# The first cycle's order on GpSimd: rows scattered ahead of the scaling of the third pair

## The chip, the cores and the metric

The kernel runs on one core of a Trainium2 chip. A core has TensorE (PE), VectorE (DVE), ScalarE (ACT), GpSimd (POOL) and SyncE (SP), which run on their own and wait for one another on semaphores. The metric is the device time of one launch in microseconds; lower is better.

## What is computed

The input x has 16 images of 256 channels and 32x32 pixels. Two residual blocks follow one another, each on a group-normed x (in short):

```
x = x + L0(gn(x))      # mixture of small experts gives one scale per channel: x * sigmoid(...)
x = x + L1(gn(x))
L1: x_ssm, res, gate = split(silu(in_proj(x)))     # 768 x 256 matrix
    xf  = silu(conv3(x_ssm))                        # along the 1024 tokens
    dt, B, C = dbc(xf)                              # per head
    permute tokens by a Mobius-mapped order (per head); selective scan, 8 states; permute back
    out = silu(out_proj(y * silu(gate) + res))
```

L0 and both norms come down to one factor and one shift for each image and channel, so that the input of L1 is x * P + B in place. The order of the tokens depends on the head alone, and is computed at run time as a table of row numbers, `idx`.

## The kernel before

The 16 images are worked in 8 pairs (`PH = 8`, two images each). Three buffers hold pairs (`xb0` to `xb2`, pair i in `xb[i % 3]`). Each engine has its own program, written out by hand, and the order of instructions on an engine is the order of the code. There is no scheduler. After a prologue (statistics of all images, ranks of the tokens, the first pairs' projections) each engine runs `cycle(i)` for i from 0 to 7. Cycle i finishes pair i and prepares pairs i+1 and i+2. What it does around the change:

- POOL scales x of pair i+2 in place (`scale_x`, L443, two instructions per image). It needs the parameters of that pair (`pcur_ready`, set by DVE at L1027, `take_params`) and the loaded x (`x_in`). It signals `x_scaled` once per image.
- POOL scatters the rows of pair i+1 to DRAM in the permuted order (`scatter`, L462, 16 indirect DMAs of 128 rows of 290 floats). It needs `stage_ready`, which DVE gives with the last of three `add_bias` (L1046) on the tile `stage`, and the earlier reads of the same DRAM rows.
- `scattered` makes POOL wait until all the scattered rows have landed. SP waits for the same (`store_c`, L352), and then loads the permuted rows of pair i+1 back (`load_rows`, L362, L370, L372). DVE begins `softplus` (L1065) of pair i+1 from them.
- POOL gathers the results of pair i from DRAM in the original order (`gather`, L476, 8 indirect DMAs per head), after SP has stored that head's results (`store_y`, L389). PE turns them with `turn_back` (L1547).
- PE projects pair i+2 (`project`, L1429), first one image and then the other, and waits for `x_scaled` before each. Then come six of the eight units of `residual` of pair i (also L1429), `turn_back` of head 0 mixed with the last two units, `turn_back` of head 1 and the output projection (L1557).
- ACT drains the projection (L627) and applies the first tap (L634); DVE adds two more taps (`convolve`, L1040).

In cycle 0 alone the parameters of pairs 2 to 7 aren't there at its start. They are the end of a chain on DVE, PE and ACT (`rescaled`, `group_variance`, `scaled`, `biases`) inside cycle 0, which ends in `take_params(2)`. In a later cycle, `take_params` stands at the head of DVE's cycle.

Of the kernel before, what the change touches and what calls it, by code (L numbers as in the profile page):

```python
# [29 lines left out]
NB = 2  # L30
# [68 lines left out]
def build(nc, x_d, w1g_d, b1g_d, w2_d, b2_d, inw_d, inb_d, dww_d, dwb_d, dbcw_d, dbcb_d, alog_d,  # L99
          alogt_d, dpar_d, mob_d, outw_d, outb_d, const_d, out_d):  # L100
    with ExitStack() as ctx:
# [6 lines left out]
        def v(tensor, off, *dims, parts=P, p0=0):  # L108

            width = tensor.shape[1]  # L110
            assert off + sum(step * (count - 1) for step, count in dims) < width
            return bass.AP(tensor, p0 * width + off, [[width, parts]] + [list(d) for d in dims])
# [173 lines left out]
        def x_loads(i):  # L286

            return 16 * (1 + i // XB)
# [19 lines left out]
        def x_view(par, b, ct, off=0, n=N):  # L308
            return v(xb[par], (b * CT + ct) * N + off, (1, n))
# [113 lines left out]
        def _(pool):  # L423

            def hold(semaphore, value):

                if isinstance(value, int) and value <= 0:
                    return
                pool.wait_ge(semaphore, value)
                pool.sem_inc(pool_passed, 1)  # L430

            def scale_x(i, images=range(NB)):

                if i < NB:
                    hold(scales_ready, 1)
                else:
                    hold(pcur_ready, i + 1)
                par = i % XB
                for b in images:
                    hold(x_in[par][b], x_loads(i))  # L440
                    params = v(pcur, (par * NB + b) * PRM_W, (1, PRM_W))
                    for ct in range(CT):
                        last = nc.gpsimd.tensor_scalar(x_view(par, b, ct), x_view(par, b, ct),  # L443
                                                       params[:, PRM_P + ct:PRM_P + ct + 1],
                                                       params[:, PRM_B + ct:PRM_B + ct + 1], ALU.mult, ALU.add)
                    last.then_inc(x_scaled, 1)

            def scatter(i):
                for nt in range(NT):

                    if nt % BIAS_TILES == 0:

                        hold(stage_ready, i * BIAS_U + 2 + nt // BIAS_TILES)
                    if nt == 0:

                        hold(dbc_rows_in, 16 * (1 + H) * i)
                        for h in range(H):
                            hold(x_rows_in[h], 16 * i)
                        hold(c_stored, 16 * i)
                    for h in range(H):  # L460
                        k = h * NT + nt
                        pool.indirect_dma_start(  # L462
                            out=xt_d.ap(), out_offset=bass.IndirectOffsetOnAxis(ap=idx[:, k:k + 1], axis=0),
                            in_=v(stage, (nt * H + h) * ROW, (1, ROW)), in_offset=None).then_inc(rows_scattered, 16)

            def scattered(i):
                hold(rows_scattered, 256 * (i + 1))

            def gather(i, h):
                hold(y_stored[h], 48 * (i + 1))  # L470
                if h == 0:

                    hold(w_ready, H * (i + 1))
                for nt in range(NT):
                    k = h * NT + nt
                    pool.indirect_dma_start(  # L476
                        out=v(crow, k * NB * P, (1, NB * P)), out_offset=None, in_=yt_d.ap()[0:(h + 1) * N],
                        in_offset=bass.IndirectOffsetOnAxis(ap=idx[:, k:k + 1], axis=0)).then_inc(y_gathered[h], 16)
                if h == H - 1:
                    hold(y_gathered[0], 128 * (i + 1))  # L480
                    hold(y_gathered[1], 128 * (i + 1))

            def cycle(i):
                if i < PH - 2:
                    scale_x(i + 2, (0,))
                if i < PH - 1:
                    scatter(i + 1)
                if i < PH - 2:
                    scale_x(i + 2, (1,))
                if i < PH - 1:  # L490
                    scattered(i + 1)
                for h in range(H):
                    gather(i, h)
# [39 lines left out]
            for i in range(PH):  # L533
                cycle(i)
# [1182 lines left out]
```

## Time and profile before

| | us |
|---|---|
| median of 3 runs (lowest, highest) | 838.59 (837.87, 839.11) |
| the profiled execution, its own time | 842.28 |
| its span | 840.5 |
| PE busy in the span | 735.4 (88%) |
| DVE busy | 592.7 (71%) |
| ACT busy | 508.6 (61%) |
| POOL busy | 354.4 (42%) |

The span runs from the first instruction to the last. Cycle 0 lies at about 120 to 235 us. From 245 us on the cycles repeat every 88 us, and PE is busy for 85.3 of them. Issuing instructions of DMAs count as busy on POOL alone. Times in the rows below are us from the start of the span, and a number in brackets is idle time ahead of the row and what ended it. A fp32 matmul of 512 columns has two records in the trace, so that one image's projection (4 units of 2 matmuls) stands as x16 and six units of the residual as x24.

### The profile page before, as it was taken

How to read it: one execution, taken by the hardware profiler on the slowest of the kernel's cores; microseconds unless marked ns; L12 is line 12 of the kernel's file. 1: busy time of each engine (PE TensorE's matmuls, PEld its weight loads, DVE VectorE, ACT ScalarE, POOL GpSimd, SP SyncE). 2: the span in 40 equal slices, each digit the busy share in tenths (PEclk: the TensorE clock that was granted, in tenths of full speed). 3: DMA queues.
4: the chain of work that ended last, by engine and by line, in shares of the span. 5: the costliest groups of instructions: out<-in, count | busy, mean ns of one | idle time of the engine just before them, and what ended most of it. 6: DMA issues, size and time to landing. Idle time of an engine off the chain costs nothing.

```text
span 840.5 us, 11680 instructions
## 1 busy us (share of the span) xinstructions
PE 735.4 (88%) x4190; PEld 435.9 (52%) x4190; DVE 592.7 (71%) x1097; ACT 508.6 (61%) x954; POOL 354.4 (42%) x325
## 2 busy tenths in 40 slices
PE   2599867929999999999999999999999999697976
PEld 1356556614566456545755565546654566354642
DVE  5699589624787578957894779577957786378533
ACT  5775745426764875488467756676667764544422
POOL 2295300377038711873087407760577037600330
PEclk9699857969999999999999999999999999998989
DMA  9924550248464937484747564765568434942332
GB/s 329 369 101 165 143 128 1 83 134 212 107 213 144 245 87 246 136 215 120 219 143 189 164 183 156 190 194 131 195 191 213 115 131 142 254 114 87 110 92 100
DMA packets 128539, 136.40 MB, mean 162 GB/s; under 512 B 57305, under 2 KB 107106, under 8 KB 126434
## 3 DMA queue, kind: packets, MB, share of 16 engines
q1 hardware_dynamic: 114448, 99.42, 41.3%
q0 software_dynamic: 12288, 35.80, 13.1%
q10 hardware_dynamic: 1746, 0.45, 0.3%
q8 instruction: 33, 0.54, 0.3%
q14 instruction: 24, 0.20, 0.1%
HBM read 83.08 MB, written 53.61 MB: 163 GB/s over the span
## 4 chain that ended last, share of the span: by engine, by line
POOL 28%; PE 20%; DMA 19%; DVE 15%; issue 13%; ACT 4%; SPq 0%; POOLq 0%; DVEq 0%; ACTq 0%
POOL xt_scratch L462 15%; POOL crow L476 11%; DMA out<-xb 7%; PE pj L1557 7%; PE pj L1429 5%; DMA xb<-in_x 3%; DMA crow<-yt_scratch,idx 3%; DMA xt_scratch<-stage,idx 3%; DVE xf L1040 2%; DVE rs L894 2%; PE tp L1547 2%; POOL xb L443 2%; DMA crow<-cd_scratch 1%; PE tp L1449 1%; DVE xb L1225 1%
## 5 line engine op out<-in xcount | busy, mean ns | idle before, releaser
L1429 PE MATMUL pj<-xb,inw 128*128 128x512 f32 x768 | 350.4, 608 | 21.5 <-POOL xb L443 16.0
L1429 PEld LDWEIGHTS pj<-xb,inw 128*128 128x128 f32 x768 | 144.7, 194 | 187.2 <-issue 155.9
L462 POOL DMA_INDIRECT xt_scratch<-stage,idx x128 | 152.0, 1188 | 80.9 <-issue 73.7
L476 POOL DMA_INDIRECT crow<-yt_scratch,idx x128 | 135.0, 1054 | 109.5 <-DMA yt_scratch<-rs 62.1
L443 POOL TENSOR_SCALAR xb<-xb,pcur 128x1024 f32<-128x1024 f32 x30 | 46.5, 1559 | 257.2 <-DMA xb<-in_x 170.3
L1040 DVE SCALAR_TENSOR_TENSOR xf<-xs,small,xf 128x1024 f32<-128x1024 f32 x64 | 83.9, 1322 | 76.0 <-ACT xf L634 74.5
L1557 PE MATMUL pj<-gt,outw 128*128 128x512 f32 x256 | 118.9, 596 | 0.1
L734 ACT ACTIVATE rs<-pj,small 128x512 f32<-128x512 f32 x64 | 44.2, 694 | 58.1 <-PE pj L1557 58.0
L677 ACT COPY stage<-tp 128x256 f32<-128x256 f32 x128 | 47.8, 374 | 44.9 <-PE tp L1451 42.1
L690 ACT COPY rs<-pj 128x512 f32<-128x512 f32 x64 | 33.0, 600 | 67.7 <-PE pj L1524 67.7
L703 ACT ACTIVATE gt<-pj,pcur 128x512 f32<-128x512 f32 x64 | 41.5, 687 | 46.0 <-PE pj L1429 45.9
L1449 PE MATMUL tp<-dw,xf 128*128 128x162 f32 x256 | 63.3, 331 | 4.8 <-ACT stage L678 3.9
L1557 PEld LDWEIGHTS pj<-gt,outw 128*128 128x128 f32 x256 | 46.6, 192 | 38.2 <-issue 37.4
L1225 DVE SCALAR_TENSOR_TENSOR xb<-xb,pcur,rs 128x1024 f32<-128x1024 f32 x32 | 41.0, 1284 | 35.2 <-ACT rs L734 35.2
L1449 PEld LDWEIGHTS tp<-dw,xf 128*128 128x128 f32 x256 | 46.5, 204 | 36.5 <-issue 26.8
L627 ACT ACTIVATE xs<-pj,pcur 128x512 f32<-128x512 f32 x64 | 41.7, 688 | 37.5 <-PE pj L1429 30.3
L1169 DVE TENSOR_TENSOR big<-big,crow 128x1024 f32<-128x1024 f32 x32 | 60.6, 1938 | 1.1 <-DMA crow<-cd_scratch 1.0
L1451 PE MATMUL tp<-dw,xf 128*128 128x162 f32 x256 | 59.6, 317 | 0.0
L1212 DVE TENSOR_TENSOR gt<-tp,gt 128x512 f32<-128x512 f32 x64 | 41.2, 683 | 25.9 <-PE tp L1547 25.8
L724 ACT ACTIVATE rs<-pj,pcur 128x512 f32<-128x512 f32 x56 | 36.1, 687 | 28.9 <-PE pj L1429 24.7
L1547 PE MATMUL tp<-dw,crow 128*128 128x128 f32 x256 | 36.9, 286 | 15.9 <-DMA crow<-yt_scratch,idx 13.0
L665 ACT ACTIVATE big<-sg,small 128x272 f32<-128x272 f32 x128 | 50.1, 502 | 0.2
(256 smaller groups left out, 1059.0 us busy)
## 6 DMA issues: line engine op xcount, KB each, us to landing
xb<-in_x SPq DMA_DIRECT2D x16, 1024.0 KB, 5.7
xp<-xt_scratch SPq DMA_DIRECT2D x16, 1024.0 KB, 9.6
crow<-cd_scratch SPq DMA_DIRECT2D x16, 1024.0 KB
out<-xb SPq DMA_DIRECT2D x16, 1024.0 KB, 6.4
yt_scratch<-rs SPq DMA_DIRECT2D x16, 512.0 KB, 3.6
yt_scratch<-rs SPq DMA_DIRECT2D x32, 256.0 KB, 5.4
gt<-in_x SPq DMA_DIRECT2D x4, 1024.0 KB, 12.0
big<-in_x SPq DMA_DIRECT2D x4, 1024.0 KB, 13.7
```

Of the source, the lines that this page charges most:

```text
L443: last = nc.gpsimd.tensor_scalar(x_view(par, b, ct), x_view(par, b, ct), params[:, PRM_P + ct:PRM_P + ct + 1], params[:, PRM_B + ct:PRM_B ...
L462: pool.indirect_dma_start(out=xt_d.ap(), out_offset=bass.IndirectOffsetOnAxis(ap=idx[:, k:k + 1], axis=0), in_=v(stage, (nt * H + h) * ROW ...
L476: pool.indirect_dma_start(out=v(crow, k * NB * P, (1, NB * P)), out_offset=None, in_=yt_d.ap()[0:(h + 1) * N], in_offset=bass.IndirectOffs ...
L665: last = nc.scalar.activation(v(big, s * EEW, (1, EEW)), v(sg, 0, (1, EEW)), ACT.Exp, scale=v(small, ANEG + h * S + s, (1, 1)))
L1040: nc.vector.scalar_tensor_tensor(dst, tap(k), wt(k), dst, ALU.mult, ALU.add).then_inc(conv_step[ot], 1)
L1169: nc.vector.tensor_tensor(v(big, W_OFF + b * NT * L, (Q * L, S), (L, NT), (1, L)), v(big, SEG + b * NT * L, (EEW, S), (L, NT), (1, L)), v( ...
L1225: nc.vector.scalar_tensor_tensor(x_view(par, b, ot), x_view(par, b, ot), std, v(rs, (b * CT + ot) * N, (1, N)), ALU.mult, ALU.add).then_in ...
L1429: last = nc.tensor.matmul(o[:, :], v(inw, ct * 3 * C + col + ot * P, (1, P)), x_view(par, b, ct, nt * HALF, HALF), start=(ct == 0), stop=( ...
L1449: nc.tensor.matmul(v(o, 0, (1, P + HK)), tile(0), v(dw, HK, (1, P + HK)), start=True, stop=False, skip_group_check=True)
L1451: nc.tensor.matmul(v(o, P, (1, HK + P)), tile(1), v(dw, 0, (1, HK + P)), start=False, stop=True, skip_group_check=True).then_inc(x_full, 1)
L1547: last = nc.tensor.transpose(v(o, e * P, (1, P)), v(crow, (h * NT + nq * 4 + e) * NB * P + b * P, (1, P)), const("ident"))
L1557: last = nc.tensor.matmul(o[:, :], v(outw, h * C + ot * P, (1, P)), v(gt, (b * CT + h) * N + nt * HALF, (1, HALF)), start=(h == 0), stop=( ...
```

## The change

In cycle 0 POOL scales no image ahead of the scatter. It scatters the rows of pair 1 first, and scales both images of pair 2 behind that. In all other cycles the first image is still scaled ahead of the scatter and the second behind it.

```diff
             def cycle(i):
+
+                early = 1 if i else 0
                 if i < PH - 2:
-                    scale_x(i + 2, (0,))
+                    scale_x(i + 2, range(0, early))
                 if i < PH - 1:
                     scatter(i + 1)
                 if i < PH - 2:
-                    scale_x(i + 2, (1,))
+                    scale_x(i + 2, range(early, NB))
                 if i < PH - 1:
                     scattered(i + 1)
                 for h in range(H):
```

On POOL, at the start of its cycle 0, these instructions stood in a row before (`stage` is the tile scattered, `xb` the pair's x, `x_in20` and `x_in21` the loads of pair 2's images):

```order
L462 DMA xt_scratch<-stage,idx 2048x290 x7
L443 TENSOR_SCALAR xb<-xb,pcur 128x1024 [waits pcur_ready,x_in20]
L443 TENSOR_SCALAR xb<-xb,pcur 128x1024
L462 DMA xt_scratch<-stage,idx 2048x290 [waits stage_ready,dbc_rows_in,x_rows_in0,x_rows_in1,c_stored]
L462 DMA xt_scratch<-stage,idx 2048x290 x7
L462 DMA xt_scratch<-stage,idx 2048x290 [waits stage_ready]
L462 DMA xt_scratch<-stage,idx 2048x290 x7
L443 TENSOR_SCALAR xb<-xb,pcur 128x1024 [waits pcur_ready,x_in21]
L443 TENSOR_SCALAR xb<-xb,pcur 128x1024
L476 DMA crow<-yt_scratch,idx 128x256 [waits rows_scattered,y_stored0,w_ready]
```

And these stand there now:

```order
L462 DMA xt_scratch<-stage,idx 2048x290 x7
L462 DMA xt_scratch<-stage,idx 2048x290 [waits rows_scattered,pcur_ready,stage_ready,dbc_rows_in,x_rows_in0,x_rows_in1,c_stored]
L462 DMA xt_scratch<-stage,idx 2048x290 x7
L462 DMA xt_scratch<-stage,idx 2048x290 [waits stage_ready]
L462 DMA xt_scratch<-stage,idx 2048x290 x7
L443 TENSOR_SCALAR xb<-xb,pcur 128x1024 [waits pcur_ready,x_in20]
L443 TENSOR_SCALAR xb<-xb,pcur 128x1024
L443 TENSOR_SCALAR xb<-xb,pcur 128x1024 [waits x_in21]
L443 TENSOR_SCALAR xb<-xb,pcur 128x1024
L476 DMA crow<-yt_scratch,idx 128x256 [waits rows_scattered,y_stored0,w_ready]
```

The two instructions that scale the first image have moved from ahead of the 16 scatters to behind them, and the gathers keep their place behind both. The wait for `pcur_ready` now stands twice: on the first scatter and on the first scaling. The function `scale_x` asks for `pcur_ready` ahead of its loop over images, and its call with an empty range still stands ahead of the scatter. The other engines' order is the same. Where PE takes the scaled images in its cycle 0, its rows are, before and now:

```order
L1524 MATMUL pj<-hs,cblk 128x128 x7
L1429 MATMUL pj<-xb,inw 128x512 [waits r_drained,x_scaled]
L1429 MATMUL pj<-xb,inw 128x512
L1429 MATMUL pj<-xb,inw 128x512 [waits r_drained]
L1429 MATMUL pj<-xb,inw 128x512
L1429 MATMUL pj<-xb,inw 128x512 [waits r_drained]
L1429 MATMUL pj<-xb,inw 128x512
L1429 MATMUL pj<-xb,inw 128x512 [waits r_drained]
L1429 MATMUL pj<-xb,inw 128x512
L1429 MATMUL pj<-xb,inw 128x512 [waits a_drained,x_scaled]
L1429 MATMUL pj<-xb,inw 128x512
```

The first of these is the first image of pair 2, which waits for its `x_scaled`, and the one further down is the second image, which waits for its own. Nothing moved here.

## Rows read from the trace of the kernel before

**Rows 1.** The page, part 4: the chain that ended last.
```profile
...
POOL 28%; PE 20%; DMA 19%; DVE 15%; issue 13%; ACT 4%; SPq 0%; POOLq 0%; DVEq 0%; ACTq 0%
POOL xt_scratch L462 15%; POOL crow L476 11%; DMA out<-xb 7%; PE pj L1557 7%; PE pj L1429 5%; DMA xb<-in_x 3%; DMA crow<-yt_scratch,idx 3%; DMA xt_scratch<-stage,idx 3%; DVE xf L1040 2%; DVE rs L894 2%; PE tp L1547 2%; POOL xb L443 2%; DMA crow<-cd_scratch 1%; PE tp L1449 1%; DVE xb L1225 1%
...
```

**Rows 2.** Waits, 130 to 212 us: who for whom, us, times, longest.
```profile
...
POOL xb L443 <- DVE pcur L1027: 67.1, 1, 67.1
...
PE pj L1429 <- POOL xb L443: 16.0, 1, 16.0
...
```

**Rows 3.** Timeline of POOL in cycle 0: start, duration, instruction [idle before].
```profile
...
159.66 2.37 POOL L443 TENSOR_SCALAR xb<-xb,pcur 128x1024 f32<-128x1024 f32 x2 [67.07 <-DVE pcur L1027]
162.19 1.01 POOL L462 DMA_INDIRECT xt_scratch<-stage,idx  x1 [0.16 <-issue]
...
172.35 1.92 POOL L462 DMA_INDIRECT xt_scratch<-stage,idx  x1 [0.30 <-issue]
...
180.60 0.97 POOL L462 DMA_INDIRECT xt_scratch<-stage,idx  x1 [2.48 <-issue]
...
184.40 0.96 POOL L462 DMA_INDIRECT xt_scratch<-stage,idx  x1 [0.30 <-issue]
185.40 2.36 POOL L443 TENSOR_SCALAR xb<-xb,pcur 128x1024 f32<-128x1024 f32 x2
187.92 1.01 POOL L476 DMA_INDIRECT crow<-yt_scratch,idx  x1 [0.16 <-issue]
...
```

**Rows 4.** Timeline of DVE in cycle 0.
```profile
...
134.29 0.86 DVE L1046 TENSOR_TENSOR stage<-stage,small 128x272 f32<-128x272 f32 x3
...
159.16 0.18 DVE L1027 COPY pcur<-prm 128x24 f32<-128x24 f32 x1
...
172.15 5.12 DVE L1040 SCALAR_TENSOR_TENSOR xf<-xs,small,xf 128x1024 f32<-128x1024 f32 x4 [8.57 <-ACT xf L634]
...
201.76 0.28 DVE L1065 SCALAR_TENSOR_TENSOR dts<-xp 128x16 f32<-128x16 f32 x2
...
```

**Rows 5.** Timeline of PE in cycle 0.
```profile
...
164.73 7.13 PE L1429 MATMUL pj<-xb,inw 128*128 128x512 f32 x16
187.81 19.79 PE L1429 MATMUL pj<-xb,inw 128*128 128x512 f32 x40 [15.95 <-POOL xb L443]
207.44 1.04 PE L1547 MATMUL tp<-dw,crow 128*128 128x128 f32 x8
...
```

**Rows 6.** Timeline of PE in cycle 1, the same pieces.
```profile
...
270.63 24.30 PE L1429 MATMUL pj<-xb,inw 128*128 128x512 f32 x56
294.77 1.04 PE L1547 MATMUL tp<-dw,crow 128*128 128x128 f32 x8
...
```

**Rows 7.** Windows around PE's restart: busy, PEclk, DMA share.
```profile
...
172.00:187.80 15.80, 0.00 (x0) 0.61 0.33 115
187.80:189.00 1.20, 1.19 (x2) 0.50 0.54 49
...
192.00:193.00 1.00, 1.00 (x3) 0.71 1.17 184
193.00:194.00 1.00, 1.00 (x4) 1.00 1.15 145
...
```

**Rows 8.** Timeline of POOL, the scatter of cycle 1.
```profile
...
248.48 1.04 POOL L462 DMA_INDIRECT xt_scratch<-stage,idx  x1 [0.16 <-issue]
...
253.00 3.66 POOL L462 DMA_INDIRECT xt_scratch<-stage,idx  x1 [0.30 <-issue]
...
272.08 0.96 POOL L462 DMA_INDIRECT xt_scratch<-stage,idx  x1 [0.30 <-issue]
...
```

**Rows 9.** Timeline of POOL, the scatter of the prologue.
```profile
...
71.78 1.20 POOL L462 DMA_INDIRECT xt_scratch<-stage,idx  x1 [7.26 <-DVE stage L1046]
...
91.62 0.96 POOL L462 DMA_INDIRECT xt_scratch<-stage,idx  x1 [0.30 <-issue]
...
```

**Rows 10.** DMAs that SP issues after the scatter of cycle 0.
```profile
...
186.92 0.57 SPq L352 DMA_DIRECT2D cd_scratch<-xt_scratch  x1
...
```

## The prediction, made before the changed kernel ran

> **What bounds the kernel now.** I first read the page's chain of waits [rows 1]. POOL has the largest share of it, 28%, though POOL is busy for 42% of the span, and its scatter L462 alone has 15%. So where POOL's scatter stands in the order can set the end. Then I read who waited for whom from 130 to 212 us, the stretch that the change touches [rows 2]: POOL's scaling waited 67.1 us, in one piece, for the parameters from DVE, and PE's projection waited 16.0 us, in one piece, for POOL's scaling. The timelines of POOL, DVE and PE say how the two belong together [rows 3 to 5]. DVE ends its `add_bias` of pair 1 at about 135.15 (134.29 + 0.86), so the rows to be scattered are ready then. It writes pair 2's parameters at 159.16 for 0.18 us, to 159.34. Before, POOL then scales the first image (159.66, 2.37 us), scatters from 162.19 to 185.36, and scales the second image up to 187.76. PE projects the first image from 164.73 to 171.86, stands for 15.95 us, and begins the second at 187.81, 0.05 us behind POOL. From there PE works 19.79 us without a gap up to `turn_back` at 207.44. That stall is on the path to the end: all of what follows (output, its store, the load into the freed buffer, the next scaling) hangs on it, and nothing later in the kernel is bound to a fixed time.
>
> **What the change seems to do, and what it does.** If the scatter could leave when its rows are ready, it would run from 135.2 to about 160, and PE's stall would be gone. But the moved scatter still waits for the parameters. `scale_x` asks for `pcur_ready` ahead of its loop over images. The new call has an empty range, so that it scales nothing, and the wait stays. The order in the section on the change shows it: the first scatter of pair 1 now has `pcur_ready` among its waits. What is queued behind that instruction on POOL is the whole scatter, both scalings and the gathers. So the scatter leaves at about 159.8 (159.34, plus the 0.32 us from there to POOL's start before, plus 0.16 for the step to an indirect DMA [rows 3, 4]), which is 2.4 us sooner than 162.19, the time of the one scaling that went from in front of it. For that, PE's first image, which was ready at 162.03, is ready only behind 16 scatters.
>
> **The scatter's length.** It was 23.17 us here (162.19 to 184.40 + 0.96) [rows 3]. In the prologue the same 16 took 20.80 (71.78 to 91.62 + 0.96) [rows 9], in cycle 1 24.56 (248.48 to 272.08 + 0.96) [rows 8]. In the 23.17 are two irregular things: one issue of 1.92 us in place of 0.96, at 172.35, just behind the start of DVE's L1040 at 172.15, and a gap of 2.48 in place of 0.30 at 178.12, for which the profile has no releaser. L1040 will come only after the scatter (it needs PE's projection), so I take its 0.96 off: 22.2 us. The gap I keep, since nothing tells what ends it. The ends are 20.8 and 24.6.
>
> The Trainium skill ("SBUF — State Buffer", section "Who interferes with whom") says that a VectorE instruction with two SBUF inputs contends with a GpSimd instruction that reads SBUF, "not with one that only writes it", and takes it from there that `tensor_tensor` doesn't hold up descriptor writing. By that rule L1040 isn't to blame for the 1.92 us, nothing is saved, and the sum below comes out 0.96 us higher. The trace bears the rule out only in part: an issue of 3.66 us stands at 253.00 in cycle 1 [rows 8].
>
> **The sum.** Scatter from 159.8 to 182.0. First scaling 2.37 us [rows 3], DVE being idle: 184.4. PE begins the first image 0.05 us later, at 184.45, in place of 164.73: 19.7 us later. But now it runs without a stall between the images. What PE needs from the start of the first image to `turn_back` is read in cycle 1, where nothing stalls it: 270.63 to 294.77, 24.14 us [rows 6]. The two further waits in this stretch, for ACT's drained banks and for the next image scaled, are covered: ACT was free sooner than in cycle 1, and the second image is scaled at 186.8, when PE is not halfway through the first.
>
> To this comes the clock. Before, PE idled from 172 to 187.8 and then ran at a granted clock of 0.50, the lower of the two levels (1.2 GHz), until it was back to 1.00 in the window from 193 [rows 7]: 4.2 us at 0.50 (the windows up to 192 are like the one shown) and 1 us at 0.71, which is 4.8 us at half speed, or 2.4 us lost. The other way to count gives the same: 40 records at cycle 1's pace are 40 x 24.30 / 56 = 17.36, and they took 19.79 [rows 5, 6]. PE's idle stretch is now longer, from 164.7 to 184.45, so I expect the same restart and charge the same 2.4 us.
>
> So `turn_back` begins at 184.45 + 24.14 + 2.4 = 210.99, in place of 207.44: 3.55 us later. DVE's chain moves with PE's and no more: its `softplus` L1065, at 201.76 before, is behind the second image's taps, which PE's units set. The rows that it reads are loaded by SP behind the scatter; SP issues the first of these at 186.92 [rows 10], and this moves to about 183.6, so it is no bound. The gathers begin when both images are scaled, at about 186.9 in place of 187.92 [rows 3], and are wanted 3.5 us later than before, so they are hidden. Put the other way: PE starts the pair 19.72 us later and saves the stall of 15.95 us in the middle, 3.77; the 0.2 between the two counts is that this one counts ends of matmuls, which the trace models, and the first one starts. From there on everything is the same and 3.5 us later: the profiled execution goes from 842.28 to 845.8, which stands 3.69 above the median of the runs. Taken off, the median goes from 838.59 to 842.1.
>
> **The rivals.**
> - *The scatter is short.* The gap of 2.48 us isn't met again. The prologue's scatter of 20.80 us, without such a gap, speaks for it; that nothing in its surroundings changes speaks against it. PE starts at 159.8 + 20.8 + 2.37 + 0.05 = 183.0, and the sum is +2.1; with a clock that is back sooner by half, +0.9. The time is 839.5 to 840.7, 840.1 in the middle. That is within 0.2% of no change (1.7 us, about what a measurement of this kernel can tell from none).
> - *The scatter is long.* In cycle 1 it took 24.56 us beside a busy DVE [rows 8]; here it would overlap SP's stores of head 1, and the gap may grow. Against it: DVE is idle for nearly all of it. PE starts at 186.8 and the sum is +5.9: 844.5.
> - *The wait isn't there, and the change does what it says.* This is the one that ends faster. It is decided at the scatter's first issue: if that comes at 135.2, its 24.56 us (DVE is busy then as in cycle 1) end at 159.8, the images are scaled at 162.2 and 164.6, PE keeps its start at 164.73 and runs to `turn_back` in 24.14 us without a stall or a slow clock: 188.87 in place of 207.44, 18.6 us sooner, 820.0. The point where it tips: with `turn_back` at 207.44 PE must start by 180.9, so the first issue must come by 156.3. For it speaks only that the rows are ready; against it the wait in the order and the code. A release of 159.34 is past the tipping point.
>
> **How the numbers follow.** The forecast, with scatters of 21.6 to 23.5 us, has a chance of 0.73 and a range of its own of 841.2 to 843.6. The short scatter has 0.12, the long one 0.11, the absent wait 0.04. Slower by over 0.2% (above 840.3) are the forecast, the long scatter and a small part of the short one: 0.85. Within 0.2% is most of the short one: 0.11. Faster is 0.04. The range of 839.4 to 844.8 leaves out the absent wait and the tails of the short and the long scatter.
>
> **What would show it.** Right: POOL's first L462 of cycle 0 at about 159.8, idle for some 67 us before it, released by DVE's L1027; four scalings in a row from about 182; PE's L1429 from 184.4 with some 18 to 20 us of idle time before it, as one piece of 56 records; a granted clock of 0.50 for its first 4 to 5 us; `turn_back` at about 211; cycles of 88 us from there. Wrong: a first scatter before 156 (then the time is near 820); a scatter of under 21 or over 24 us; PE's first image still at 165; or the difference at `turn_back` not found again at the end.

## Result, and the profile after

The changed kernel is slower: 843.67 us (median of 7 runs, 838.78 to 846.85) against 838.31 (median of 7, 836.26 to 839.11), ratio 1.006 with a 95% interval of 1.0032 to 1.0088. Forecast were 842.1 us and a range of 839.4 to 844.8. (The narrower range of the forecast case, 841.2 to 843.6, is missed by 0.07.) The profiled execution took 841.78 us with a span of 840.0, below the 842.28 and 840.5 of before, and still its first cycle is slower. How that goes together is told below.

The page's chain of waits, part 4, answers to [rows 1]:

```profile
...
PE 28%; POOL 24%; DMA 15%; DVE 14%; issue 11%; ACT 6%; SPq 0%; POOLq 0%; DVEq 0%; ACTq 0%
POOL xt_scratch L462 13%; POOL crow L476 10%; PE pj L1431 9%; PE pj L1559 7%; DMA out<-xb 5%; DMA xb<-in_x 3%; DVE xf L1042 2%; DVE rs L896 2%; DMA xt_scratch<-stage,idx 2%; DMA crow<-yt_scratch,idx 2%; PE tp L1549 2%; PE tp L1451 2%; DMA crow<-cd_scratch 1%; POOL xb L443 1%; ACT big L667 1%
...
```

PE now has the larger share, 28%. The restart can't be the reason: it costs 2.4 us, 0.3% of the span, and the kernel before has one too. Which engine such a chain runs over where two are nearly equal can differ between executions, so I read no cause from these shares. The waits from 130 to 215 us answer to [rows 2]:

```profile
...
POOL xt_scratch L462 <- issue: 74.9, 16, 68.2
...
PE pj L1431 <- POOL xb L443: 20.3, 1, 20.3
...
```

POOL's long wait stands on the scatter L462 now and no longer on the scaling, and PE's wait for the scaling has grown from 16.0 to 20.3 us. The timelines of POOL, DVE and PE in cycle 0 answer to [rows 3 to 5]:

```profile
...
162.22 0.96 POOL L462 DMA_INDIRECT xt_scratch<-stage,idx  x1 [68.23 <-issue]
...
172.35 0.96 POOL L462 DMA_INDIRECT xt_scratch<-stage,idx  x1 [0.30 <-issue]
...
179.50 0.97 POOL L462 DMA_INDIRECT xt_scratch<-stage,idx  x1 [2.37 <-issue]
...
183.30 0.96 POOL L462 DMA_INDIRECT xt_scratch<-stage,idx  x1 [0.30 <-issue]
184.30 4.73 POOL L443 TENSOR_SCALAR xb<-xb,pcur 128x1024 f32<-128x1024 f32 x4
189.19 1.01 POOL L476 DMA_INDIRECT crow<-yt_scratch,idx  x1 [0.16 <-issue]
...
```

```profile
...
160.76 0.18 DVE L1029 COPY pcur<-prm 128x24 f32<-128x24 f32 x1
...
194.75 2.61 DVE L1042 SCALAR_TENSOR_TENSOR xf<-xs,small,xf 128x1024 f32<-128x1024 f32 x2 [30.11 <-ACT xf L636]
...
207.57 0.28 DVE L1067 SCALAR_TENSOR_TENSOR dts<-xp 128x16 f32<-128x16 f32 x2
...
```

```profile
...
186.72 26.69 PE L1431 MATMUL pj<-xb,inw 128*128 128x512 f32 x56 [20.33 <-POOL xb L443]
213.25 1.04 PE L1549 MATMUL tp<-dw,crow 128*128 128x128 f32 x8
...
```

The parameters are written by 160.94 (160.76 + 0.18). This is 1.60 us later than before. Of it 0.49 us are there already at the end of `stage` (135.64 for 135.15), and 1.11 arise on the chain to the parameters, which took 25.30 us from there for 24.19. In a second trace of the changed kernel this chain took 24.13, so it isn't the change; all times are best taken from the parameters on. The scatter's first issue follows 1.28 us behind them. (The timeline names no releaser for it; the chain of waits, shown further down, leads from it to DVE's write of the parameters.) Its 16 issues take 22.04 us with one gap of 2.37. Four scalings stand in a row. PE waits 20.33 us and then runs its 56 records in one piece. `turn_back` begins 52.31 us behind the parameters (213.25 - 160.94), where before it was 48.10 (207.44 - 159.34): 4.2 us later. SP's first load behind the scatter comes at 185.81, for 186.92 in [rows 10], and binds nothing: DVE's `softplus` follows its own taps without a wait. The clock around PE's restart answers to [rows 7]: 0.50 up to 191 us, 0.72 in the next, and 1.00 from 192 on. The columns are busy time, count, PEclk, DMA share, GB/s:

```profile
...
187.00:188.00 1.00, 1.00 (x2) 0.50 0.81 75
...
191.00:192.00 1.00, 1.00 (x3) 0.72 0.76 169
...
```

### The profile page after: what moved, and what is told of

Read it like the earlier page. It is cut to its first block, busy times and chain, and to the rows that moved or that the text cites. A ratio compares the mean times of both kernels' runs of the same rounds, so it can differ in the third digit from the quotient of the medians.

```text
span 840.0 us, 11680 instructions
## 1 busy us (share of the span) xinstructions
PE 728.4 (87%) x4190; PEld 429.4 (51%) x4190; DVE 591.8 (70%) x1097; ACT 509.4 (61%) x954; POOL 355.1 (42%) x325
## 4 chain that ended last, share of the span: by engine, by line
PE 28%; POOL 24%; DMA 15%; DVE 14%; issue 11%; ACT 6%; SPq 0%; POOLq 0%; DVEq 0%; ACTq 0%
POOL xt_scratch L462 13%; POOL crow L476 10%; PE pj L1431 9%; PE pj L1559 7%; DMA out<-xb 5%; DMA xb<-in_x 3%; DVE xf L1042 2%; DVE rs L896 2%; DMA xt_scratch<-stage,idx 2%; DMA crow<-yt_scratch,idx 2%; PE tp L1549 2%; PE tp L1451 2%; DMA crow<-cd_scratch 1%; POOL xb L443 1%; ACT big L667 1%
## 5 line engine op out<-in xcount | busy, mean ns | idle before, releaser
L1431 PE MATMUL pj<-xb,inw 128*128 128x512 f32 x768 | 348.0, 604 | 27.3 <-POOL xb L443 20.3
L462 POOL DMA_INDIRECT xt_scratch<-stage,idx x128 | 150.5, 1176 | 150.8 <-issue 143.5
L476 POOL DMA_INDIRECT crow<-yt_scratch,idx x128 | 137.1, 1071 | 102.5 <-DMA yt_scratch<-rs 56.8
L1451 PE MATMUL tp<-dw,xf 128*128 128x162 f32 x256 | 61.6, 323 | 6.4 <-ACT stage L680 5.5
L1451 PEld LDWEIGHTS tp<-dw,xf 128*128 128x128 f32 x256 | 44.5, 196 | 38.7 <-issue 27.3
L1453 PE MATMUL tp<-dw,xf 128*128 128x162 f32 x256 | 57.5, 307 | 0.0
L726 ACT ACTIVATE rs<-pj,pcur 128x512 f32<-128x512 f32 x56 | 36.1, 688 | 29.4 <-PE pj L1431 24.6
```

Of the source, the lines that this page charges most:

```text
L462: pool.indirect_dma_start(out=xt_d.ap(), out_offset=bass.IndirectOffsetOnAxis(ap=idx[:, k:k + 1], axis=0), in_=v(stage, (nt * H + h) * ROW ...
L476: pool.indirect_dma_start(out=v(crow, k * NB * P, (1, NB * P)), out_offset=None, in_=yt_d.ap()[0:(h + 1) * N], in_offset=bass.IndirectOffs ...
L1431: last = nc.tensor.matmul(o[:, :], v(inw, ct * 3 * C + col + ot * P, (1, P)), x_view(par, b, ct, nt * HALF, HALF), start=(ct == 0), stop=( ...
L1451: nc.tensor.matmul(v(o, 0, (1, P + HK)), tile(0), v(dw, HK, (1, P + HK)), start=True, stop=False, skip_group_check=True)
L1453: nc.tensor.matmul(v(o, P, (1, HK + P)), tile(1), v(dw, 0, (1, HK + P)), start=False, stop=True, skip_group_check=True).then_inc(x_full, 1)
```

## The experiments

The differences are small beside single runs, so each trace is also read by one distance: from the end of the parameters' write in cycle 0 to the start of `turn_back` of head 0. It was 48.10 before and 52.31 after. A second distance, to the start of POOL's first scaling in cycle 1, shows what of it is carried on: 85.52 before (244.86 - 159.34), 89.63 after (250.57 - 160.94). Two jobs ran, each with its own runs of the kernel before: 839.52 us (median of 29, 834.36 to 845.00) beside the first four kernels, 838.44 (median of 17, 835.93 to 842.15) beside the last four.

**The wait alone taken away.**

```diff
             def scale_x(i, images=range(NB)):
+                if not len(images):
+                    return
```

Expected:

> The changed kernel, but the scaling of an empty range of images asks for nothing, so that cycle 0's scatter waits for its rows alone. Theory (the loss is the parameters' wait in front of the scatter): the first issue of the scatter comes at about 136, some 23 us before the parameters are written; 16 issues take 24.6 us beside a busy DVE; both images are scaled before PE wants them; PE's pair runs at about 24.1 us to turn_back, without the stall and the slow clock, 29.5 us behind the parameters in place of 48.1 before; the time falls by 18 us, to about 820. Rival (the order costs by itself, since the issues in the stretch from 135 to 160 hold up DVE's chain to the parameters): the parameters come later by up to 15 us and the time is 830 or more.

Measured: 823.57 us, ratio 0.982 (0.9765 to 0.9876). The timelines of POOL, of DVE for one of the stretched issues, and of PE:

```profile
...
136.87 0.96 POOL L465 DMA_INDIRECT xt_scratch<-stage,idx  x1 [42.79 <-DVE stage L1051]
...
151.18 2.83 POOL L465 DMA_INDIRECT xt_scratch<-stage,idx  x1 [0.30 <-issue]
...
158.97 0.96 POOL L465 DMA_INDIRECT xt_scratch<-stage,idx  x1 [2.43 <-issue]
...
163.75 4.72 POOL L446 TENSOR_SCALAR xb<-xb,pcur 128x1024 f32<-128x1024 f32 x4
...
```

```profile
...
150.88 2.29 DVE L1186 TENSOR_TENSOR big<-big,bc 128x2048 f32<-128x2048 f32 x1
...
```

```profile
...
166.17 24.30 PE L1434 MATMUL pj<-xb,inw 128*128 128x512 f32 x56 [0.70 <-POOL xb L446]
190.31 1.04 PE L1552 MATMUL tp<-dw,crow 128*128 128x128 f32 x8
...
```

The scatter leaves at 136.87, released by DVE's write of `stage`, and runs beside DVE's chain. That chain isn't held up: from the end of `stage` to the end of the parameters it took 24.13 us (135.91 to 160.04), for 24.19 before. It is the scatter that is held up: its 16 issues took 26.85 us, for 24.6 forecast. The distance to `turn_back` is 30.27 us, 17.8 less than before and 22.0 less than after, and the second distance is 67.61, 17.9 less than before. So the order pays and the wait is what costs. The rival is out. The median stands 3.6 us above the forecast of 820, of which the trace has 0.8 (30.27 for 29.5).

**Both images ahead of the scatter.**

```diff
-                early = 1 if i else 0      # the changed kernel
+                early = 1 if i else NB     # this one
```

Expected:

> The kernel before, with both images of cycle 0 scaled ahead of the scatter. PE's stall of 16 us between the images must go. Theory (what counts is when the scatter and the gathers behind it are through, PE's stall is only the first wait on that path): the scatter ends at about 187.7 and the gathers at about 209 as before, PE waits for the gathers in front of turn_back in place of the scaling, and the time is within 1 us of before (837.5 to 838.5). Rival (PE's stall itself is the path): turn_back of head 0 comes 18 us sooner and the time falls to about 820.

Measured: 839.04 us, ratio 1.0001 (0.9975 to 1.0027), as the theory said. PE's timeline and its waits:

```profile
...
164.09 24.30 PE L1431 MATMUL pj<-xb,inw 128*128 128x512 f32 x56
203.15 1.97 PE L1549 MATMUL tp<-dw,crow 128*128 128x128 f32 x8 [14.75 <-DMA crow<-yt_scratch,idx]
204.91 3.62 PE L1431 MATMUL pj<-xb,inw 128*128 128x512 f32 x4
...
```

```profile
...
DVE dts L1067 <- DMA xp<-xt_scratch: 12.6, 1, 12.6
...
```

PE's stall between the images is gone, and a wait of 14.75 us for the gathers stands in its place; DVE waits 12.6 us for the rows that SP can load only behind the scatter. What has to come sooner is the scatter. PE's stall on the scaling was the first of several waits on it. The distance to `turn_back` misleads here: it is 44.43 us (203.15 - 158.72), 3.7 less than before, while the second distance is 84.78, only 0.7 less. PE has restarted at the lower clock (3.62 us for four records, for 1.88 elsewhere), and what follows is bound by more than the first `turn_back`.

**The tipping point.**

```diff
             def cycle(i):
+                if not i:
+                    hold(scales_ready, 2)     # with the wait above taken away
```

Expected:

> The changed kernel, with cycle 0's scatter released by the earlier of the two parameter signals (the scales, written about 3.1 us before the biases that the scaling waits for). Theory (the delay of the scatter's first issue passes one for one to PE's start and to the end): the first issue, PE's start and turn_back all come about 3.1 us sooner against the parameters' last write than in the changed kernel; turn_back 49.2 us behind it, against 52.3 in the changed kernel and 48.1 before; the time is 1 us above before. Rival (the scatter's length absorbs it, as its irregular gap ends at a fixed time): turn_back stays at 52.3.

Measured: 843.31 us, ratio 1.0043 (1.0013 to 1.0073). POOL and PE:

```profile
...
158.18 0.95 POOL L465 DMA_INDIRECT xt_scratch<-stage,idx  x1 [64.14 <-issue]
...
176.71 0.97 POOL L465 DMA_INDIRECT xt_scratch<-stage,idx  x1 [3.66 <-issue]
...
```

```profile
...
183.93 27.30 PE L1436 MATMUL pj<-xb,inw 128*128 128x512 f32 x56 [18.54 <-POOL xb L446]
211.06 1.04 PE L1554 MATMUL tp<-dw,crow 128*128 128x128 f32 x8
...
```

The first issue came 1.80 us ahead of the parameters' end (159.98), in place of 1.28 behind it: 3.1 us sooner, as meant. PE started 23.95 us behind the parameters in place of 25.78, so 1.8 us were passed on, and `turn_back` came at 51.08, 1.2 us sooner. The gap at the thirteenth issue took 3.66 us in place of 2.37, and PE's slow restart took 27.30 us for the 56 records in place of 26.69. The second distance is 88.67, 1.0 less than in the changed kernel. The time forecast, 1 us above before, isn't met: the median is 3.8 above. This is neither the theory nor the rival in full: the gap isn't at a fixed time, but it isn't of a fixed length either.

**PE kept busy in its stall.**

```diff
+                if not i:
+                    pe.wait_ge(x_drained, 2 * X_U)
+                    for k in range(22):
+                        nc.tensor.matmul(tp[k % 2][:, :], v(inw, 0, (1, P)), v(inw, 0, (1, HALF)), start=True, stop=True)
                 if beyond:
                     for b in range(NB):
```

Expected:

> The changed kernel, with 22 idle matmuls of 512 columns (about 19 us, their result isn't read) on PE in cycle 0's stall. Theory (2.4 us of the loss is the restart of PE at the lower granted clock): the granted clock is 1.00 when the pair's projection begins, the 56 records take 24.3 us in place of 26.7, turn_back comes 49.9 us behind the parameters in place of 52.3, and the time is 2.4 us below the changed kernel's. Rival (the slow start has another cause, such as cold banks or the chain of ACT and DVE behind the first image): 26.7 us and 52.3 us stay.

Measured: 841.97 us, ratio 1.0046 (1.0018 to 1.0074). PE's timeline:

```profile
...
163.69 19.15 PE L1617 MATMUL tp<-inw 128*128 128x512 f32 x44
184.13 24.30 PE L1431 MATMUL pj<-xb,inw 128*128 128x512 f32 x56 [1.30 <-POOL xb L443]
208.27 1.04 PE L1549 MATMUL tp<-dw,crow 128*128 128x128 f32 x8
...
```

The pair's records take 24.30 us and `turn_back` is at 49.94, both as forecast to a tenth. The granted clock was 1.00 from 163.7 us on, and so the 2.4 us of the clock term are shown. Against the 48.10 of before, 1.84 us are left, and 2.06 at the second distance (87.58). In whole times the gain isn't shown. The median is 2.5 above before here, and it was 5.0 and 5.4 above for the changed kernel, a difference of the right size; but the ratio, 1.0046, isn't below the 1.006 and 1.0044 of the changed kernel by more than the intervals allow.

**The changed kernel and the one without the wait, once more.**

Expected, of the changed kernel and of the one without the wait:

> The changed kernel once more. Theory (all of its loss arises in cycle 0, and the rest of its first measurement was the clock of single executions in the last cycles): 4.2 us above before, ratio 1.005. Rival (something behind cycle 0 adds to it): 1.006 or more again, with a difference in the trace behind 245 us that is there in each execution.

> The kernel without the wait once more, for its distance from the changed kernel and from the next two on one chip. By the traces so far turn_back of cycle 0 is 17.8 us nearer to the parameters than before and 22.0 us nearer than in the changed kernel: about 17 us below before, ratio 0.979 to 0.982.

Measured: the changed kernel 843.48 us, ratio 1.0044 (1.0021 to 1.0067); without the wait 818.17 us, ratio 0.9762 (0.9731 to 0.9794). PE of the changed kernel, again:

```profile
...
185.45 26.41 PE L1431 MATMUL pj<-xb,inw 128*128 128x512 f32 x56 [20.28 <-POOL xb L443]
211.69 1.04 PE L1549 MATMUL tp<-dw,crow 128*128 128x128 f32 x8
...
```

The parameters were at 159.74, so `turn_back` is at 51.95, 3.9 us above before. The ratio of 1.0044 is 3.7 us, against 3.9 in the trace; the medians alone stand 5.0 us apart, 1.0060, which the interval holds as well. The trace has no further loss up to cycle 5: POOL's scaling there starts 3.9 us later against the parameters than before (441.50 for 437.56). So the theory is borne out by the trace, and the times don't exclude one more microsecond. Without the wait the ratio lies a little below the forecast of 0.979 to 0.982.

**The last cycle's waits filled.**

```diff
+            def fill(i, count):
+                if i == PH - 1:
+                    pe.wait_ge(y_drained, i * Y_U)
+                    for k in range(count):
+                        nc.tensor.matmul(tp[k % 2][:, :], v(inw, 0, (1, P)), v(inw, 0, (1, HALF)), start=True, stop=True)
...
+                fill(i, 2)           # before the second chunk_sums of head 0
+                fill(i, 3)           # before within of head 0
+                fill(i, 6)           # before turn_back
```

Expected:

> The kernel without the wait, with 11 idle matmuls of 512 columns (2, 3 and 6) on PE in the three longest waits of the last cycle. Theory (the run-to-run differences and some of the time of the last 90 us are PE's granted clock, which falls at these waits): the granted clock is 1.00 from the first filled wait to the end, the 16 transposes behind the last wait take 2.1 us in place of 3.9, the time falls by 3 to 5 us against the kernel without the wait, and single runs lie closer together. Rival (what ends last there are the gathers and ACT, and PE's clock has slack): within 1 us.

Measured: 819.52 us, ratio 0.9773 (0.9747 to 0.9798). Its six runs lie within 1.0 us (819.14 to 820.13), those of the kernel without the wait in the same job within 5.9 (817.15 to 823.08). PE at the end without the fill, and with it:

```profile
...
796.55 3.94 PE L1552 MATMUL tp<-dw,crow 128*128 128x128 f32 x16 [5.63 <-DMA crow<-yt_scratch,idx]
...
```

```profile
...
782.74 5.31 PE L1571 MATMUL tp<-inw 128*128 128x512 f32 x12
...
793.85 1.10 PE L1552 MATMUL tp<-dw,crow 128*128 128x128 f32 x8 [0.61 <-DMA crow<-yt_scratch,idx]
...
```

The clock stayed at 1.00 up to the end of PE's work, as meant, and the transposes are short. The profiled execution is 3.4 us shorter in its span (817.8 for 821.2), but the one that it is compared with was among the two longest of its six. The median isn't lower, so the forecast of 3 to 5 us is missed and the rival, within 1 us, isn't excluded.

In this job the kernel without the wait has runs on both sides: the four with a mean granted clock of 0.954 or more took 817.15 to 818.73, the two with 0.946 took 823.03 and 823.08. It isn't a rule: in the first job its run with 0.957 took 823.97 us and the one with 0.952 took 821.73. Nor does the fill by itself make runs agree. The next kernel has the same fill, and its six runs lie 4.6 us apart (817.82 to 822.37). That the spread between runs is PE's clock in the last cycle is therefore not shown.

**The first image behind 14 of 16 scatters.**

```diff
+                if not i:                            # beside the fill of the one before
+                    scatter(1, range(NT - 1))
+                    scale_x(2, (0,))
+                    scatter(1, (NT - 1,))
+                    scale_x(2, (1,))
+                elif i < PH - 1:
                     scatter(i + 1)
```

Expected:

> The same as the one with the filled end, and in cycle 0 the first image is scaled behind 14 of the 16 scatters, the second behind all. In the kernel without the wait PE waited 0.70 us for the first scaling. Theory: PE's pair starts right behind the last use of its banks, 0.7 us sooner; the gathers start as before and are hidden; 0.7 us are gained, which is at the edge of what can be measured. Rival: the last two scatters' rows now come 2.4 us later and DVE's softplus waits for them; no gain or a loss of up to 2 us.

Measured: 819.54 us, ratio 0.9771 (0.9743 to 0.9800), no different from the one with the filled end. PE:

```profile
...
167.92 24.30 PE L1439 MATMUL pj<-xb,inw 128*128 128x512 f32 x56
...
```

The first image is scaled from 162.12 to 164.50 and PE no longer waits for it, but `turn_back` stands at 30.98 us behind the parameters (192.05 against 161.07), where the others had 30.2 to 30.3. Ahead of the pair PE ran at the lower clock for longer in this execution, which the window shows (busy, count, PEclk, DMA share, GB/s):

```profile
...
160.00:168.00 8.00, 8.00 (x103) 0.57 0.22 76
...
```

Whether that is chance, one trace doesn't tell. Inconclusive, and no gain.

## Why the prediction was right

**The wait in front of the scatter.** Right, and it is the whole sign of the result. By the rows to be scattered alone the forecast would have been 820.0, and with the wait gone it was 823.57 and 818.17 in two jobs.

**The scatter's first issue.** The one term that was clearly mis-sized. I put it 0.46 us behind the parameters; it was 1.28. The chain of waits of the changed kernel from 155 to 216 us, in order of time, shows what stands there (start, duration):

```profile
...
160.76 0.19 DVE pcur L1029
160.99 0.08 issue
161.09 0.08 issue
161.28 0.08 issue
161.37 0.08 issue
161.47 0.74 issue
162.22 0.96 POOL xt_scratch L462
...
```

Behind the wait for the parameters POOL still passes the scatter's own waits, one after the other, all long satisfied. Before, these steps and the start of an indirect DMA lay beside a scaling of 2.37 us. The wait that moved in front of them took away their cover, which costs 0.8 us. That is my reading of the chain, and no run takes these waits away. The other traces fit: the first issue came 1.27 us behind the parameters in two more in which it waits for them, and 0.96 us behind `stage` in the kernel without the wait (135.91 to 136.87).

**The scatter's length.** 22.2 forecast, 22.04 here. The issue of 1.92 us at 172.35 [rows 3] is 0.96 in each of the four traces in which DVE's taps come only behind the scatter, that is two of the changed kernel, the tipping point and the busy PE. That the prediction blamed the taps was right, and the traces say more exactly what holds an issue up. The 1.92 us ended at 174.27, 0.83 us behind the end of the first of DVE's four taps (172.15, and 1.29 long). The 3.66 us of cycle 1 [rows 8] ended at 256.66, 0.83 behind this pair:

```profile
...
251.98 3.85 DVE L1169 TENSOR_TENSOR big<-big,crow 128x1024 f32<-128x1024 f32 x2
...
```

And the 2.83 us in the kernel without the wait ended at 154.01, 0.84 behind L1186 (153.17). So it is throughout: of the 2560 issues in the ten traces 478 took 1.1 us or more, and 467 of these ended 0.81 to 0.86 us behind a DVE instruction with two inputs in SBUF. An issue that begins at least 0.1 us into such an instruction, with 0.3 us or more of it still to come, was stretched in 410 cases of 410. Where one of the two inputs is in PSUM, the banks that PE writes (`cblk<-sg,cst` of 128x1024, the issue at 263.05) it was in none of 65. With both images ahead the taps and the issues overlap too, and each issue took 0.96 to 1.00. There it began within 0.03 us of a tap's start, or with at most 0.17 us of a tap left. No run was made for this, so it is read from the timing alone.

The Trainium skill ("SBUF — State Buffer", section "Who interferes with whom") says that a VectorE instruction with two SBUF inputs contends with a GpSimd instruction that reads SBUF, and infers that `tensor_tensor` doesn't hold up descriptor writing. The traces speak against the inference: such instructions hold up the issue of an indirect DMA, by up to 2.7 us in the row at 253.00.

**The gap.** Kept, and it was there, 2.35 to 2.48 us in nine of the ten traces of this case and 3.66 in one, each time in front of the thirteenth issue of cycle 0's scatter, the 29th of the program. It began at times from 156 to 179 us, and with none, two or four scaling instructions ahead of the scatter. So it doesn't go with the time. It goes with the count of indirect DMAs; a cause in POOL's program near this place, which these kernels shift by four instructions at most, isn't excluded. What it is stays open.

**PE's pair.** 24.14 + 2.4 = 26.54 from its start to `turn_back`; measured 26.53 (186.72 to 213.25), and 24.14 with the clock kept up. The clock term is shown by experiment.

**The sum.** +3.55 forecast to `turn_back`; +4.2 and +3.9 in two traces. Of the difference of the first to the forecast, 0.8 is the first issue, and 0.2 the shorter scatter with the other sign. The medians moved by 5.4 and 5.0, the ratios say 1.006 and 1.0044, whose intervals hold 1 + 3.55 / 838.3 = 1.0042. That a median lands 1.6 us from the forecast is no proof of the sum, since the runs of the changed kernel spread by 7 to 8 us; it is the distances inside the traces that bear the sum out.

**"From there on everything is the same."** Right up to the last two cycles, and false for a single execution in them: the profiled execution was forecast at 845.8 and took 841.78. The stall of PE, which the prediction put on the path to the end, was on it only as one of several waits on POOL, as the kernel with both images ahead shows; in the changed kernel it is the last of them. Against the parameters the gathers begin 0.3 us sooner there than before (28.25 us behind them for 28.58), and `turn_back` 4.2 us later, so the sum holds. POOL's scaling in cycle 1 starts at 250.57 here and at 244.86 before, 5.7 us later (4.1 and the 1.6 by which the parameters came later). It is 5.8 us later in cycle 5, at 602.72. Then the profiled execution of before lost what the one after did not. PE in the last cycle, before:

```profile
...
754.01 1.09 PE L1481 MATMUL st<-xp,bblk 128*64 128x128 f32 x16
...
758.87 1.70 PE L1481 MATMUL st<-xp,bblk 128*64 128x128 f32 x16 [2.46 <-DVE hs L1113]
...
773.70 1.99 PE L1512 MATMUL pj<-xp,mblk 64*64 64x128 f32 x32 [3.23 <-ACT gt L703]
...
791.79 2.10 PE L1524 MATMUL pj<-hs,cblk 64*128 64x128 f32 x32 [0.22 <-DVE hs L1122]
...
```

And after:

```profile
...
758.61 1.09 PE L1483 MATMUL st<-xp,bblk 128*64 128x128 f32 x16
...
763.24 1.09 PE L1483 MATMUL st<-xp,bblk 128*64 128x128 f32 x16 [2.25 <-DVE hs L1115]
...
776.44 1.10 PE L1514 MATMUL pj<-xp,mblk 64*64 64x128 f32 x32 [1.61 <-ACT gt L705]
...
791.80 2.10 PE L1526 MATMUL pj<-hs,cblk 64*128 64x128 f32 x32 [0.21 <-DVE hs L1124]
...
```

The distance from the first to the last of these is 37.8 us before and 33.2 after. In the first PE's matmuls run slow behind the waits (1.70 for 1.09, 1.99 for 1.10), in the second they don't: from 754 to 765 and from 765 to 780 us the granted clock was 0.84 and 0.77 before, and 1.00 in both after. The waits are longer too (3.23 for 1.61), and what made the two executions part isn't shown. It isn't the change, for in the second trace of the changed kernel the same distance is 36.7 us. These 4.6 us are why the spans of two single executions compare the wrong way round. One execution of each would have told the opposite of the truth, and by the profile's own span the changed kernel would have won.

**The rivals.** The short and the long scatter didn't come. The absent wait didn't come by itself, and was made by hand; it brought 16 and 20 us in the medians and 17.8 in the trace, where 18.6 were worked out.

## What to carry to other kernels

A wait that a helper asks for ahead of its loop stays when the loop is empty. Before an order is judged, read in the compiled order which waits stand on the instruction that was to move up. Where an engine has a long run of issues, what it waits for at its head counts for everything behind it, so ask which single wait is the last to come, and whether the first of the run needs it. And where single executions differ by more than the change is worth, compare distances inside the traces, from the last event that the change can't touch to the first that all depends on, and check one further on: with both images ahead `turn_back` began 3.7 us sooner and the time was the same.

The version to keep is the one without the wait: 818.17 and 823.57 us in two jobs, 1.8% to 2.4% below the kernel before.

## What the runs showed that was not expected

The runs of the kernel before spread much wider in the first job (29 runs, 834.36 to 845.00) than in the three runs at the start (837.87 to 839.11), with mean granted clocks from 0.937 to 0.953. The three runs of 0.951 and more took 834.36 to 835.08, and the slowest, 845.00, had 0.938. The order isn't strict: of two runs with 0.949 one took 834.65 and one 838.85. With eleven idle matmuls in the last cycle six runs agreed within 1.0 us in one kernel and within 4.6 in another.

The sixteen issues of one scatter took 22.04 us with DVE idle, and 26.85 (136.87 to 162.76 + 0.96) beside DVE's work in cycle 0, since a DVE instruction with two SBUF inputs holds up an issue that begins during it. Filling PE's wait with idle matmuls kept the granted clock at 1.00 over 20 us and cost nothing that the profile shows: they ended 1.3 us before PE's wait did.
